# A graph network's row gathers, without the memset behind each one and with the group's last gather counting its own end

## The reference

```python
def _rgcn_layer(x, W, SW, b, src, dst, rel):
    xt = jnp.einsum('nd,rde->rne', x, W)
    msg = xt[rel, src]
    agg = jax.ops.segment_sum(msg, dst, num_segments=x.shape[0])
    return jax.nn.relu(agg + x @ SW + b)
...
x = _layernorm(x + rgcn(rgcn(x)))
feat = jax.nn.relu(x @ W1 + b1)
h = feat * d_invsqrt
agg = jax.ops.segment_sum(h[src], dst, num_segments=N)
x = _layernorm(x + (feat - agg * d_invsqrt) @ W2 + b2)
```

## Time and profile before

| what | value |
| --- | --- |
| median of three runs | 7370.4 us (7354.83 to 7371.55) |
| span of the profiled execution, first to last instruction | 7320.2 us |
| around the span, against the median | 50.2 us |
| POOL busy | 5851.5 us, 80% of the span |
| PE busy | 3691.2 us, 50% |
| DVE busy | 1720.1 us, 23% |
| ACT busy | 409.6 us, 6% |
| 16 DMA engines, share busy in nearly all slices | 0.1 to 0.2 |

### The profile page before, as it was taken

The page is one execution under the profiler, slowest core; times in us unless marked ns, Lnnn a source line. Parts: engine busy times, 40 slices in busy tenths (PEclk is TensorE's granted clock), DMA queues, the critical chain, the costliest instruction groups (busy, mean ns, idle before and its releaser), DMA issues.

```text
span 7320.2 us, 56431 instructions
## 1 busy us (share of the span) xinstructions
PE 3691.2 (50%) x13687; PEld 2669.6 (36%) x13841; DVE 1720.1 (23%) x2844; ACT 409.6 (6%) x915; POOL 5851.5 (80%) x9940
## 2 busy tenths in 40 slices
PE   4555555555555556556565555554424333433343
PEld 3333333333333333334343333433323333333333
DVE  4333333333333212222222222221101111111111
ACT  1000000000000100000000000010000000000000
POOL 7888888888888588888888888867888888888887
PEclk7666667676666777767677776675555555555555
DMA  2111111111111112211222221211111111111111
GB/s 66 49 51 52 50 50 50 51 52 50 50 52 51 40 49 57 56 56 55 56 58 56 56 57 56 56 54 42 51 51 52 51 51 51 51 51 53 51 51 48
DMA packets 197585, 382.88 MB, mean 52 GB/s; under 512 B 84322, under 2 KB 93326, under 8 KB 197542
## 3 DMA queue, kind: packets, MB, share of 16 engines
q0 software_dynamic: 159456, 326.88, 17.0%
q1 hardware_dynamic: 36416, 54.67, 2.1%
q10 hardware_dynamic: 1670, 0.85, 0.0%
HBM read 356.43 MB, written 25.65 MB: 52 GB/s over the span
## 4 chain that ended last, share of the span: by engine, by line
POOL 48%; issue 20%; another core or an unknown queue 20%; PE 7%; DVE 3%; DVEq 1%; POOLq 0%; ACT 0%; DMA 0%; ACTq 0%; SPq 0%
POOL rows L794 39%; POOL pause L798 9%; PE bank L980 3%; PE bank L950 3%; DVE r_S L1042 1%; DVE r_hot L1037 1%; PE bank L1205 1%; ACT r_agg L904 0%; PE bank L1440 0%; PE bank L964 0%; DVE acc L1081 0%; DMA acc<-in_dst_dram 0%; DVEq L1071 0%; POOLq L109 0%
## 5 line engine op out<-in xcount | busy, mean ns | idle before, releaser
L794 POOL DMA_INDIRECT rows<-in_x_dram,idx x1661 | 1588.6, 956 | 466.9 <-issue 396.7
L794 POOL DMA_INDIRECT rows<-x_d,idx x1647 | 1574.2, 956 | 453.5 <-issue 397.8
L794 POOL DMA_INDIRECT rows<-h_d,idx x1640 | 1566.9, 955 | 441.4 <-issue 396.3
L980 PE MATMUL bank<-r_S,rows 128*128 128x128 f32 x6644 | 1408.2, 380 | 705.1 <-issue 486.8
L1205 PE MATMUL bank<-r_S,rows 128*128 128x64 f32 x3322 | 821.9, 388 | 1332.3 <-issue 1079.4
L980 PEld LDWEIGHTS bank<-r_S,rows 128*128 128x128 f32 x6644 | 1299.5, 285 | 501.4 <-issue 482.1
L1205 PEld LDWEIGHTS bank<-r_S,rows 128*128 128x128 f32 x3322 | 775.1, 315 | 1378.0 <-issue 1272.4
L798 POOL MEMSET pause<- 128x128 f32 x4948 | 1096.3, 222 | 4.3 <-issue 0.2
L1042 DVE TENSOR_TENSOR r_S<-bank,key 128x1792 f32<-128x1792 f32 x238 | 480.4, 2019 | 1225.9 <-remote 1080.3
L964 PEld LDWEIGHTS bank<-zeros_bf 128*128 128x128 bf16 x476 | 54.1, 114 | 1463.0 <-issue 1056.8
L964 PE MATMUL bank<-zeros_bf 128*128 128x512 bf16 x323 | 174.9, 542 | 722.4 <-issue 505.8
(11 more groups left out here) (152 smaller groups left out, 1471.1 us busy)
## 6 DMA issues: line engine op xcount, KB each, us to landing
rows<-in_x_dram,idx POOLq DMA_INDIRECT x1661, 3.3
rows<-x_d,idx POOLq DMA_INDIRECT x1647, 3.4
rows<-h_d,idx POOLq DMA_INDIRECT x1640, 3.4
d_xr<-in_x_dram SPq DMA_DIRECT2D x54, 218.0 KB
x_d<-d_yr SPq DMA_DIRECT2D x27, 218.0 KB
d_x1r<-x_d SPq DMA_DIRECT2D x27, 218.0 KB
h_d<-d_hr SPq DMA_DIRECT2D x27, 218.0 KB
part_d<-d_pr SPq DMA_DIRECT2D x27, 218.0 KB
```

Of the source, the lines that this page charges most:

```text
L794: pool.indirect_dma_start(out=self.c.rows[:, self.place(s), :], out_offset=None, in_=self.table[:, :], in_offset=bass.IndirectOffsetOnAxis ...
L980: mm = pe.matmul(agg_ps[j][:, bass.ds(offs[j * KG + k], TK)], c.rows[:, g.place(h * KG + k), :], S[:, pb, j * KG + k, :], start=False, sto ...
```

## The change

The memset behind each gather and its scratch tile go.

```diff
-        c.pause = sb("pause", [P, PT, P])
...
-        self.paused = sem("paused")
+        self.written = sem("written")
...
                     if h % rest == 0:
-                        pool.wait_ge(self.paused, q * (NG // rest) + i * (RING // rest) + h // rest + 1)
+                        pool.wait_ge(self.written, q * (NG // rest) + i * (RING // rest) + h // rest + 1)
                         gate(pool, self.c.passed)
                     for k in range(part.of(h)):
                         s, slot = h * KG + k, h if k < halves(part, h) else RING + h % PAIR
                         if s < skip:
                             continue
+                        closes = k == part.of(h) - 1 and h % rest == rest - 1
                         pool.indirect_dma_start(
                             out=self.c.rows[:, self.place(s), :], out_offset=None, in_=self.table[:, :],
                             in_offset=bass.IndirectOffsetOnAxis(ap=self.c.idx[:, at + s:at + s + 1], axis=0)
+                            engine_sem=self.written if closes else None
                         ).then_inc(self.landed[slot], 16)
-                        ins = pool.memset(self.c.pause[:, s % PT, :], 0.0)
-                    if h % rest == rest - 1:
-                        ins.then_inc(self.paused, 1)
```

More of the change, by code:

```diff
@@ L776, in iteration @@
                 if (p + 1) * PT <= skip:
-                    pool.sem_inc(self.paused, PAIR // rest)
+                    pool.sem_inc(self.written, PAIR // rest)
                     continue
@@ L784, in iteration @@
                         if h % rest == rest - 1:
-                            pool.sem_inc(self.paused, 1)
+                            pool.sem_inc(self.written, 1)
                         continue
                     if h % rest == 0:
-                        pool.wait_ge(self.paused, q * (NG // rest) + i * (RING // rest) + h // rest + 1)
+                        pool.wait_ge(self.written, q * (NG // rest) + i * (RING // rest) + h // rest + 1)
                         gate(pool, self.c.passed)
@@ L793, in iteration @@
                             continue
+                        closes = k == part.of(h) - 1 and h % rest == rest - 1
                         pool.indirect_dma_start(
                             out=self.c.rows[:, self.place(s), :], out_offset=None, in_=self.table[:, :],
-                            in_offset=bass.IndirectOffsetOnAxis(ap=self.c.idx[:, at + s:at + s + 1], axis=0)
+                            in_offset=bass.IndirectOffsetOnAxis(ap=self.c.idx[:, at + s:at + s + 1], axis=0),
+                            engine_sem=self.written if closes else None
                         ).then_inc(self.landed[slot], 16)
-                        ins = pool.memset(self.c.pause[:, s % PT, :], 0.0)
-                    if h % rest == rest - 1:
-                        ins.then_inc(self.paused, 1)
         def one_round(q, skip=0):
@@ L828, in run @@
         pool.end_ifs()
-        pool.wait_ge(self.paused, rounds * (NG // rest) + 1)
+        pool.wait_ge(self.written, rounds * (NG // rest) + 1)
         gate(pool, self.c.passed)
```

## The result

| | before | changed |
| --- | --- | --- |
| median of four runs | 7366.3 us (7354.83 to 7371.55) | 7480.4 us (7471.21 to 7490.22) |
| span of the profiled execution | 7320.2 us | 7488.3 us |
| changed over before | | 1.0156 (95%: 1.0140 to 1.0172) |

The forecast was 7000 us with a range of 6890 to 7180. It was wrong in sign. What came is rival C's kind, at about half of the pairs' heads.

What follows compares the result with a forecast made beforehand. POOL's own pace of gathers and memsets, busy 80%, was taken to bound the kernel. Span 7320.2 - 450 (own pace) + 10 (not on the path) + 70 (stops) = 6950, with 50 around it 7000 us; range 6890 to 7180.

Steps and rivals of the forecast that it cites:

- rival C: Slower: other engines' crawl takes over, POOL stops 2.5 us at every pair's head before PE gets instructions; 7740 us, 7%.
- Within a group: Between a group's gathers on POOL: dropping the memset wins 0.088 us to each gather, the rest returning as longer idle.
- At a head: From a group's last gather to the next: 0.11 us won, between 0 and 0.22, depending on when the gather's count comes.
- The sum of POOL's own pace: Gains within groups and at heads over all three rounds: 450 us won, bounds 385 to 515.
- Rivals D and E: D: the count comes only with the rows' landing, 8305 us, 3%. E: the change does nothing, 2%.
- What is not on the path: At the rounds' starts and ends: POOL's faster pace wins nothing while it waits for others; 10 us lost.
- The reading of the earlier trace: Two SP semaphore instructions of 698 ns near back-to-back gathers were held against hidden instruction fetch; the 70 us was kept.
- Stops: POOL's waits, mostly at pairs' heads, while other engines crawl: about 70 us before, taken to double, 70 us more.
- Around the span: Outside the profiled span: 50 us added, as the median stands to the span.

Runs made afterwards that it cites:

- e14_three_quarters: The kernel before with a memset of 128x96 in place of 128x128 behind each gather; 7312.2 us, 1.0116 of before.
- e2_last: The kernel before with only the memset behind a group's last gather (round 3: a pair's last) left; 7433.9 us, 1.0124 of before.
- e7_head: The kernel before with memsets only at heads: one behind an even group's last gather, six in a row behind a pair's last; 7384.9 us, 1.0052.
- g0_none: The changed kernel with the gathers of the loops left out; 3225.8 us, 0.4519 of before.
- e9_half: The changed kernel with gathers of 256 bytes a row in place of 512; 7444.7 us, 1.0309 of before.
- g3_64: The changed kernel with gathers of 64 rows in place of 128; 6429.8 us, 0.9007 of before.
- h96_rows: The changed kernel with gathers of 96 rows in place of 128; 7419.7 us, 1.0270 of before.
- g1_half: The changed kernel with three gathers of a group in place of seven; 3515.1 us.
- g2_memsets: The changed kernel with seven memsets of 128x18 in place of each gather; 3488.9 us.
- e6_two: The kernel before with two memsets of 128x64 behind each gather in place of one of 128x128; 7298.0 us, 1.0102 of before.

## Why the prediction was wrong, point by point

**Within a group** (0.088 us to each gather): right. The gathers between the rounds showed what comes of a gather right behind a gather: 1.252 us there, 1.248 now.

**At a head** (0.11, bounds 0 and 0.22): right within its bounds, at the upper one. The idle behind the counting gather is 0.80, the count comes with its bar's end. The sum of POOL's own pace was 450, with bounds of 385 to 515; it is 538. Rivals D and E fall with these two rows, and so does the reason for the middle value. The Trainium skill (Perfetto Trace Analysis, DMA Instruction, SWDGE) leaves open who posts a further count; the rows of the changed kernel show that here `engine_sem` is up within 0.80 us of the bar's end, before a landing could be (3.3 us at the least from issue).

**What is not on the path** (10 us): too small. The edges of the rounds cost 134. I took the waits between the rounds as fixed, since they hang on the last tail; but the last tail hangs on PE, and PE is now behind POOL by as much as the buffer holds. This term failed too, and for the same reason: with the stops it makes up the 706 us that came in place of the 80.

**The reading of the earlier trace rows.** The prediction takes two instructions of 698 ns as a sign that the fetch of instructions is not hidden. They show late instructions, and not that a fetch made them late.

**Stops** ("From 0 to four times as much; I take a doubling, +70 us"): this is the step that failed. They rose from 84 to 656 us, nearly eightfold, outside the bounds that I gave. The mechanism was named rightly: the others' instructions crawl, POOL uses up its lead, stops, and they go on. I had priced rival C by a stop of 2.5 us at every pair (7740) and gave its decisive point as 180 of 356 pairs; what came is 159 stops that are 4.1 us longer than the usual idle. What misled me is the reading of rounds 1 and 2: that POOL was within 9 us of its own pace there I took as room. It was the contrary. The others kept up just so, at an edge which the trace of before can't show, because an engine that keeps up looks the same with much room and with none. PE at 50% busy said nothing on that either. A run on another chip shows how near the edge is: with 0.19 us less a group (e14_three_quarters) the stops go from 60 to 186 us, the idles between the rounds from 25 to 94, and the kernel is slower by 1.2%.

**Around the span** (50 us): the profiled execution of the changed kernel, with a span of 7488.3, is the one of 7490.22 us; 1.9 us lie outside. So the 50 us were not launch time: the profiled execution of before was itself a shorter one than the median. What made the others longer, more stops perhaps, is not shown, as only one was profiled on that chip. The term is small against the miss.

**Is the cause settled?** Shown: the loss is POOL's waits at heads and at the rounds' edges for work of PE and what hangs on it (the sum closes to 1 us); it comes from POOL's faster mean pace and not from the new count (e2_last, e7_head); PE and the others could do their work in 3226 us (g0_none), so it is not their own work that bounds them. Not shown in general is that they get their instructions only when POOL stops: it is so at 61 of 94 long pieces of PE here, but at 26 of 78 with the same kernel on the other chip.

Open is what sets off the crawl. It is not the bytes (e9_half), not the gathers' packets and bytes together (g3_64 beside e9_half), not rows per us (h96_rows), not the density of gathers by itself (g1_half), and not POOL's activity at half its time (g2_memsets). It was seen only with gathers of 96 rows or more, one to each tile that PE works on, at 1.34 us apart or less; that 1.36 us is free of it rests on the two kernels with the many instruction transfers. The last six runs each left out other things as well (g1_half halves the gathers to a tile, g3_64 touches half of the partitions), and which of these matters was not tried.

The nearest guess would be that the fetch of instructions is held up. The Trainium skill (Runtime: NRT & Kernel Launch, Instruction fetch mechanics) has instruction fetch hidden behind the issue of instructions, and nothing here speaks against that. The trace of the changed kernel has no instruction transfer from 319 to 2485 us, from 2830 to 4995 and from 5310 to 7460, but 146 of the 159 stops, 78 of the long pieces and 627 of the 683 instructions of PE that started 0.69 to 0.71 us after the one before (583 before, 8 in g0_none) stand in just these stretches. Where such transfers go on all along (e6_two), the crawl is all but gone. Nor is it PE's loop jumping back: behind each of its 90 branches PE's next instruction starts within 0.3 us. So, as far as the trace records the transfers, a fetch that comes late is not the cause; what holds the instructions that are already there is unknown.

## What to carry to other kernels

An engine that just keeps up with the one that bounds the kernel is no proof of room: before forecasting a gain from a faster bound, find out what the follower could do alone (here one run without gathers) and how its pace depends on the leader's. A filler instruction behind each transfer may be a throttle in effect: make its size a parameter and measure both sides of it, for here 0.18 us more in a group cost 1.0% and 0.19 us less 1.2%. And if the expected waits are priced from a trace in which they are rare, the range must reach to where they are the rule.

## What the runs showed of the hardware that was not expected

- Two memsets of 128x64 in a row take 0.25 us together at 168 ns each, six of 128x128 take 0.95 us at 224 each: GpSimd's memsets overlap.
- A gather's bar hardly depends on its rows: 905 ns for 64, 923 for 96, 935 for 112, 944 for 128; with half the bytes 944 too.
- While the crawl lasts, PE's instructions start at multiples of 0.70 us, with no transfer of instructions in the trace. In the piece shown ACT got going 0.1 us behind POOL's stop, PE 0.8, DVE 3.9.
- Gathers of 64 rows, 1.208 us apart, leave the others alone; gathers of 96 rows, 1.23 us apart, do not: 0.9007 of the time of before against 1.0270. Gathers of 128 rows with half the bytes, in the same packets and bytes as those of 64 rows, do not either: 1.0309.
- The kernel before took 7140 to 7366 us in the six comparisons; the changed one, with more stops, varied less in its two (7433 and 7480).
